# Layer stage: the weighted values of both sequences in one phase of 32 small products, and the scores of a later tile directly behind it

## The reference

```python
for i in range(DEPTH):                                   # DEPTH = 6
    x = attn_layer(shift_tokens(x), Wqkv[i], q_scale[i], k_scale[i], Wo[i]) + x
    x = ffn_layer(shift_tokens(x), ln_g[i], ln_b[i], W1[i], b1[i], W2[i], b2[i]) + x

def attn_layer(x, Wqkv, qs, ksc, Wo):                    # 16 heads of 64
    q, k, v = split(x @ Wqkv)
    q = l2norm(q) * qs ; k = l2norm(k) * ksc             # then rotated by position
    sim = q k^T * 8 ; sim = where(mask, -max, sim)       # a query sees itself and 32 before it
    out = softmax(sim) @ v
    return out @ Wo
```

## Time and profile before

| | us |
|---|---|
| median of 3 runs | 4349.85 (4349.69 to 4352.57) |
| profiled execution, first to last instruction | 4352.3 |
| busy: TensorE / weight loads | 4168.5 / 3088.7 |
| busy: VectorE / ScalarE / GpSimd | 3653.6 / 3390.6 / 2644.6 |
| layer stage | roughly 480 to 3440 |

### The profile page before, as it was taken

How to read it: one execution, slowest core, us unless ns; L and a number is a source line. 1 busy time by engine, 2 the same in 40 slices (tenths; PEclk the granted TensorE clock), 3 DMA queues, 4 the chain that set the end, 5 groups by cost and what they waited for, 6 DMA issues and landing times.

```text
span 4352.3 us, 150350 instructions
## 1 busy us (share of the span) xinstructions
PE 4168.5 (96%) x61520; PEld 3088.7 (71%) x61520; DVE 3653.6 (84%) x11101; ACT 3390.6 (78%) x9585; POOL 2644.6 (61%) x2210
## 2 busy tenths in 40 slices
PE   7999989999999999999999999999999889999999
PEld 5777756666666666666666666666666578888888
DVE  4665689999999999999999999999999566776765
ACT  3545478989999899989999899989999556666665
POOL 3444477777777777777777777777777333333331
PEclk9888799999999999999999999999999889999999
DMA  3000000000000000000000000000000100000000
GB/s 103 4 4 4 5 2 4 4 4 4 29 4 3 4 29 4 4 4 4 29 4 4 4 29 3 4 4 9 26 7 7 33 2 4 4 4 4 4 4 6
DMA packets 65256, 46.40 MB, mean 11 GB/s; under 512 B 29220, under 2 KB 63032, under 8 KB 63800
## 3 DMA queue, kind: packets, MB, share of 16 engines
q1 hardware_dynamic: 64568, 36.78, 3.0%
HBM read 28.48 MB, written 2.10 MB: 7 GB/s over the span
## 4 chain that ended last, share of the span: by engine, by line
PE 77%; DVE 12%; ACT 8%; issue 2%; POOL 1%; SPq 0%; DMA 0%; DVEq 0%; POOLq 0%; ACTq 0%
PE ps L564 63%; PE ps L568 14%; DVE BIG L1126 5%; ACT BIG L907 4%; ACT BIG L915 3%; DVE sm L1137 3%; DVE BIG L1134 1%; POOL BIG L1587 1%; DVE BIG L1131 1%; ACT ps L907 1%; DVE sm L1134 0%; DVE BIG L1204 0%; DVE BIG L1130 0%; DVE rs L1126 0%; DVE x_sb L1126 0%
## 5 line engine op out<-in xcount | busy, mean ns | idle before, releaser
L564 PE MATMUL ps<-WB,BIG 128*128 128x128 f32 (+2 forms) x8576 | 1988.2, 366 | 48.0 <-DVE BIG L1134 41.0
L907 ACT ACTIVATE BIG<-ps 128x512 f32<-128x512 f32 (+5 forms) x3168 | 1446.8, 514 | 535.5 <-PE ps L568 347.2
L1587 POOL TENSOR_TENSOR BIG<-BIG,sm 128x512 f32<-128x512 f32 (+1 forms) x864 | 1223.0, 1425 | 720.0 <-DVE sm L1338 536.6
L564 PEld LDWEIGHTS ps<-WB,BIG 128*128 128x128 f32 (+1 forms) x8576 | 1132.6, 192 | 274.9 <-issue 151.3
L1587 POOL TENSOR_TENSOR BIG<-BIG 128x512 f32<-128x512 f32 x768 | 966.4, 1278 | 93.1 <-DVE BIG L1126 92.8
L568 PEld LDWEIGHTS ps<-t_ident,BIG 128*128 128x128 f32 x6016 | 726.6, 146 | 353.4 <-issue 251.0
L564 PEld LDWEIGHTS ps<-BIG 64*64 64x64 f32 (+2 forms) x37888 | 648.8, 131 | 458.9 <-issue 273.5
L568 PE MATMUL ps<-t_ident,BIG 128*128 128x128 f32 x6016 | 911.9, 283 | 53.6 <-DVE BIG L1126 24.0
L1137 DVE TENSOR_REDUCE sm<-BIG 128x8 f32<-128x512 f32 (+3 forms) x1472 | 879.8, 613 | 37.8 <-ACT BIG L915 35.1
L564 PE MATMUL ps<-BIG 64*64 64x64 f32 (+4 forms) x37888 | 812.2, 227 | 64.5 <-ACT BIG L907 19.4
L1590 POOL TENSOR_TENSOR sm<-sm,halfn 128x1 f32<-128x1 f32 (+2 forms) x336 | 290.5, 871 | 744.7 <-DVE sm L1130 410.2
(11 more groups left out here) (121 smaller groups left out, 3027.8 us busy)
## 6 DMA issues: line engine op xcount, KB each, us to landing
WB<-in_Wqkv SPq DMA_DIRECT2D x6, 1536.0 KB, 6.9
XS<-y_sb SPq DMA_DIRECT2D x96, 63.0 KB
y_sb<-in_ctx SPq DMA_DIRECT2D x16, 256.0 KB, 3.2
WB<-in_Wo SPq DMA_DIRECT2D x6, 512.0 KB, 8.1
x_sb<-in_x SPq DMA_DIRECT2D x8, 256.0 KB, 5.1
WB<-in_F_W SPq DMA_DIRECT2D x1, 2048.0 KB, 9.1
WB<-in_F_W SPq DMA_DIRECT2D x8, 256.0 KB, 5.0
out<-x_sb SPq DMA_DIRECT2D x8, 256.0 KB, 2.3
```

What stands on the lines that cost most here:

```text
L564: return te.matmul(o, l, r, start=start, stop=stop, skip_group_check=not check)
L907: return se.activation(o, i, ACT.Copy)
L1587: return pe_.tensor_tensor(o, a, b, op)
```

## The change

The two phases y and w become one phase y of 32 small products. It goes through both halves of the heads, and for each small product pair takes both sequences; bank y0 now holds what comes from sequence half 0 (partitions 0 to 63), and y1 what comes from half 1, both halves of the heads in each. The wait of w for y goes. ScalarE's `o0` and `o1` wait for y and each writes into the OT of both halves (`c_OT`), so TensorE's `o` waits for both copies at its start. In TensorE's list `q1` moves ahead of `y`, and `s` to directly behind `y`, ahead of `k0`, `x`, `v1` and `tr`. The lists of the other engines stay.

```diff
 C_ORDER = {
-    "pe": "1b06 1a06 2g26 2a26 1v06 1b16 2a18 2g16 1a16 1y8 1q14 1w8 1k04 1x3 1v15 2tr5 1s6 1p07 2g07 1k14 1o8 1p17 "
+    "pe": "1b06 1a06 2g26 2a26 1v06 1b16 2a18 2g16 1a16 1q14 1y8 1s6 1k04 1x3 1v15 2tr5 1p07 2g07 1k14 1o8 1p17 "
...
+        def c_OT(u):
+
+            n = 2 * (NT * u.at["l"] + u.at["t"]) % 6
+            two = BIG[:, 10240 + 2048 * n:14336 + 2048 * n].rearrange("p (f c) -> p f c", f=2)
+            return two[:, :, 512:1024].rearrange("p f (g c) -> p f g c", c=128)
...
-                elif ph in "yw":
+                elif ph == "y":
 
                     for m in ("p0", "v0", "p1", "v1"):
                         w.wait_ge(*u.on("act", m))
-                    if ph == "w":
-                        w.wait_ge(*u.on("pe", "y"))
-                    for i in range(8):
-                        hp, par = i // 2, i % 2
-                        for hf in range(2):
-                            b, K, bb = c_bufs(u, hf), bank[u.bank[f"y{hf}"]], (hf + (ph == "w")) % 2
-                            q, r = slice(64 * bb, 64 * bb + 64), half(hf, par)
-                            o = mm(K[64 * par:64 * par + 64, 256 * bb + 64 * hp:256 * bb + 64 * hp + 64],
-                                   b.VV[q, 64 * i:64 * i + 64], b.PT[q, 128 * hp + r.start:128 * hp + r.stop])
+                    for hf in range(2):
+                        b = c_bufs(u, hf)
+                        for i in range(8):
+                            hp, par = i // 2, i % 2
+                            c, r = 256 * hf + 64 * hp, 128 * hp + half(hf, par).start
+                            for bb in range(2):
+                                q = slice(64 * bb, 64 * bb + 64)
+                                o = mm(bank[u.bank[f"y{bb}"]][64 * par:64 * par + 64, c:c + 64],
+                                       b.VV[q, 64 * i:64 * i + 64], b.PT[q, r:r + 64])
                     o.then_inc(u.name("pe", ph, sems), 1)
                 elif ph == "o":
+                    w.wait_ge(*u.on("act", "o0"))
+                    w.wait_ge(*u.on("act", "o1"))
                     for hf in range(2):
-                        w.wait_ge(*u.on("act", f"o{hf}"))
                         b = c_bufs(u, hf)
...
                 elif ph[0] == "v":
                     w.wait_ge(*u.on("pe", ph))
                     if three:
-                        w.wait_ge(*three.on("pe", "w"))
+                        w.wait_ge(*three.on("pe", "y"))
...
                 elif ph[0] == "o":
-                    w.wait_ge(*u.on("pe", "w"))
-                    o = copy(b.OT.rearrange("p (g b i) -> p b g i", b=2, i=64), K.rearrange("p (b g i) -> p b g i", b=2, i=64))
+                    w.wait_ge(*u.on("pe", "y"))
+                    o = copy(c_OT(u)[:, :, :, 64 * int(h):64 * int(h) + 64], K.rearrange("p (f g i) -> p f g i", f=2, i=64))
```

More of the change, by code:

```diff
@@ L434, in build @@
                 u.after["y"] = u.after["y0"] + u.after["y1"]
-            elif u.kind == "C2" or ph != "w":
+            else:
                 take(u, ph, EMPTIED[u.kind[1] + ph], 1, 6)
```

## The result

| | before | after |
|---|---|---|
| median, us | 4349.77 (4348.19 to 4352.57, 4 runs) | 4510.56 (4508.53 to 4516.79, 4 runs) |
| ratio, 95% interval | | 1.0372 [1.0358, 1.0386] |
| first to last instruction, us | 4352.3 | 4506.7 |
| plain period, us | 58.76 | 62.29 |
| s(A) to s(B), s(B) to s(C), s(C) to s(D), s(D) to s(A) | 12.62, 11.02, 11.28, 23.84 | 14.42, 12.79, 11.30, 23.77 |

The changed kernel is slower by 160.8 us, where 84 were forecast: the sign and the loop through ScalarE came true, the size was little more than half of what was measured. 4510 lies outside the range of 4388 to 4480.

The account below looks back on a forecast made before the run. TensorE and a loop (s, TensorE to k1 or p0, ScalarE to next mask, s) bound it. TensorE's 56.1 + 4.7 idle = 60.8 a period, +2.04; 71 + 8 + 5 = 84 gives 4434 us, range 4388 to 4480.

Parts of the forecast that it names:

- the loop through ScalarE: s, TensorE up to k1 or p0, 8.2 to 9.4 us of ScalarE to the mask, next s; earlier s lengthens it.
- The loop's three spans: s(A) to s(B), s(B) to s(C), s(C) to s(D): forecast 14.40, 12.74, 11.23, with TensorE idle 4.7 a period.
- The gain of fewer runs: Runs of small products on TensorE fall from 11 to 5 a period; at 0.35 each, about 2.1 saved.
- The banks turn differently ... 0 to 0.2 a period: p0 (g0 in slot A) takes q1's bank and waits for VectorE's work on it: 0 to 0.2 a period.
- The prediction's own sign: If TensorE's idle time names VectorE, the banks were misread; a plain period over 62 us is wrong.
- Here TensorE counts ... 22.4: s(D) to s(A): TensorE's work sets this span, which falls from 23.84 to 22.4.
- layer 0: Its eight periods, at 60.26, gain between +0.5 and the full 2; +1 each taken as the nearer end: 8.
- layer ends and the stage's end: Five periods holding a layer's end, at 63.53, gain 0 to 2 each; 1 taken: 5.
- 1 (TensorE the only bound): Rival: the loop isn't a bound; period 56.1, faster, 4225 to 4260 us; 5%.
- 2 (half the loop): Rival: s(C) to s(D) stays at TensorE's 10.1, rest as forecast; period 59.7, about 4390 us; 9%.
- 4 (gain and loop cancel): Rival: gain and loop cancel within 0.2% (8.7 us), time unchanged; 3%.
- 3 named the right engine: Rival: stalls bring the clock to 1.2 GHz, or VectorE adds a wait; 4482 us (1 more a period) or 4530; 13%.

Follow-up runs that it names:

- Experiments 1: Kernel before, with only s moved to directly behind w, y and w still two phases, banks in the old order; 4481.01 us, ratio 1.0289.
- 6: Kernel with y joined alone, with s moved one step ahead of v1 and tr, behind k0 and x; 4399.58 us, ratio 1.0132 to before.
- 7: Changed kernel, with the exponentials of half the heads in 4 instructions of 128 columns in place of 8 of 64; 4406.62 us, ratio 1.0147 to before.
- experiment 2: Changed kernel with the old order except that w is gone: y joined, q1 behind it, s behind tr; 4336.15 us, ratio 0.9960 to before.
- experiment 3: Also called banks_y_first: changed kernel, but y takes its two banks ahead of q1, as before the change; 4467.47 us, ratio 1.0254 to before.
- 4: Kernel before, with only q1 taking its bank ahead of y's two, order of work unchanged on every engine; 4381.29 us, ratio 1.0080.
- 5: Changed kernel with s put back behind tr, q1 still ahead of the joined y; 4362.38 us, ratio 1.0042 to before.

## Why the prediction was right in kind and wrong in size

**What bounds the kernel: right.** TensorE at 298.80 of 300 was not the only bound. The waits of after (1.80, 1.77, 1.11 and 1.24) leave 56.4 of its 62.29 to TensorE's own work, against 56.1 forecast: it had some 2 us less to do, and with ScalarE's order untouched the period grew. Experiments 1 and 6 lengthen the loop, 7 shortens it, and the period follows each time.

**The loop's three spans: right.** 14.40, 12.74, 11.23 forecast; 14.42, 12.79, 11.30 measured. Together 0.14 off.

**The gain of fewer runs: right in size where it can be seen** (2.03 for the run of 128; 0.36 in s(C) to s(D) in experiment 2). But it bought less elsewhere: see the second step below.

**The step that failed: "The banks turn differently ... 0 to 0.2 a period".** It was the right wait at a wrong size. I sized it in slot A alone, where g0 takes the bank, 2.98 after s. In slot E there is no s; p0 itself takes the bank, 3.0 after y's start (2064.58 to 2067.60), while VectorE ends q1 4.2 after it. It costs 1.24 as a wait in the trace of after, 0.92 by experiment 3, 0.90 by 4 and 0.98 by 5. The wait is 1.24 and the worth is 0.92, because with it gone small waits for VectorE show. The prediction's own sign named the step: TensorE's idle time names VectorE (46.8 us), and the period is over 62.

**A second, smaller one, in the same span: "Here TensorE counts ... 22.4".** I took s(D) to s(A) as TensorE's work alone. Without the bank's wait the period is still 61.37, that is 0.57 over 60.8, of which 0.46 lies in this span (22.86 by its timeline). Experiment 2 shows the same: of a gain of 0.70 in this span 0.64 was eaten, 0.52 of it by one wait for ScalarE. Where another engine is only a few tenths behind, TensorE can't gain 1.05.

**The sum.** The profiled spans differ by 154.4, forecast 84. Between the first and last period's marker (47 distances) 152.1 of it lies so:

| | forecast | measured |
|---|---|---|
| plain periods | 35 x 2.04 = 71 | 36 at +3.53, six of them longer still: 132.5 |
| layer 0 | 8 x 1 = 8 | 5 distances at +1.4 to +2.1: 9.8 |
| layer ends and the stage's end | 5 | 3.8 + 6.0 |

In layer 0 the full 2.1 came in four of the five distances, not the nearer end that I took. Of the 77 us missed the bank's turn is 0.92 x 41 = 38 (36 plain periods and five of layer 0), the rest of s(D) to s(A) about 0.46 x 36 = 17, and the six longer periods some 6. (The ratios, each on its own chip, differ by 1.0372 - 1.0254 = 0.0118, some 51 us, but banks_y_first has none of the six either.) One thing about the layer ends the prediction left out: in before, the granted clock falls to 0.50 there (at one of them from 1471.70 to 1475.10), in after it stays at 1.00 at all four ends between the markers. So 63.53 held some 1.7 us lost to the slow clock, an estimate from half of that stretch, which after no longer pays.

**The rivals.** 1 (TensorE the only bound) and 2 (half the loop) are refuted by the three spans, 4 (gain and loop cancel) by the ratio. 3 named the right engine ("VectorE ... falls out of step and adds a wait of its own") with 13% and priced 4482 for 1 us more a period, but not the reason: most of what VectorE adds (0.92) goes once the banks turn as before (experiment 3). Its half on the clock came true in one plain period of 36 (last section). My range ended at 4480, where this rival began: with the bank term bounded in every slot it would have reached past it.

## What to carry to other kernels

Where two in-order engines feed each other in a loop, a phase moved ahead is paid for by everything that it puts between the other engine's inputs; add up the loop, not the fullest engine's busy time. When an order changes, list for every slot kind who gets whose buffer and set its new start beside the end of the old reader; here one slot of five held the whole price, two phases with their places in the turn swapped, worth 0.9 us in 60. And try the harmless half of a change by itself: it gained 0.4% where the whole lost 3.7%.

## What the runs showed of the hardware that was not expected

In five plain periods of the changed kernel (four from 700 to 3400, one at 3457.95) TensorE stops inside the run of 128 records for 0.5 to 0.9 us with no releaser ("issue"; 0.32 to 0.74 as the view counts), and the period is 0.6 to 1.0 longer; its timeline:

```profile
1197.95 2.10 PE L570 MATMUL ps<-BIG 64*64 64x64 f32 x125
1200.36 0.33 PE L570 MATMUL ps<-BIG 64*64 64x64 f32 x3 [0.32 <-issue]
...
1260.88 1.98 PE L570 MATMUL ps<-BIG 64*64 64x64 f32 x118
1263.60 0.39 PE L570 MATMUL ps<-BIG 64*64 64x64 f32 x10 [0.74 <-issue]
```

The stops come in pairs one period apart, behind 125 and then 118 records of the run, and the pair comes again after 1128 us (1200.36, 2328.72, 3457.95). The kernel with y joined alone, whose runs have at most 64 records, has no such row from 700 to 3400; banks_y_first, with runs of 128, has none either, and before has one of 0.60 among its transposes (2096.59). So the long run is not enough for a stop, nor needed for one. The cause stays open.

In a sixth period the granted clock fell: four projection records behind s(B), which had waited 1.73, take 3.45 to the next start, where four of them take 1.82 at full clock (2031.08 to 2032.90). They ran near 1.2 GHz, and the period took 1.7 more. The windows view has 0.62 for the stretch:

```profile
2657.50:2662.00 4.50, 4.50 (x48) 2.27 (x41) 4.30 (x9) 0.91 (x2) 4.50 (x4) 0.62 0.01 4
```

It happened once with 129 waits for the mask from 700 to 3400. It came directly behind a wait of 1.73, but whether the wait brought it no run here separates.
